# Batch norm factors and bias sums made by GpSimd while the count table is filled, the row factors spread by a matmul in the first pass

## The reference

```python
def _bn(h, gamma, beta, mean, var):
    return (h - mean) * (gamma * jax.lax.rsqrt(var + BN_EPS)) + beta
for i in range(L):                                   # L = 3
    agg = jax.ops.segment_sum(h[src], dst, num_segments=N)
    h = h + agg
    h = jnp.maximum(_bn(h @ W1[i] + b1[i], g[i, 0], be[i, 0], rm[i, 0], rv[i, 0]), 0.0)
    h = h @ W2[i] + b2[i]
    h = jnp.maximum(_bn(h, g[i, 1], be[i, 1], rm[i, 1], rv[i, 1]), 0.0)
```

## Time and profile before

| | us |
|---|---|
| median of 3 runs | 4120.48 (4119.42 to 4122.16) |
| the profiled execution, its own time | 4127.06 |
| its span, first to last instruction | 4125.4 |
| PE busy | 3764.2 (91%) |
| DVE busy | 3059.2 (74%) |
| ACT busy | 2492.8 (60%) |
| POOL busy | 1375.4 (33%) |

### The profile page before, as it was taken

The page is one execution under the profiler, slowest core; times in us unless marked ns, Lnnn a source line. Parts: engine busy times, 40 slices in busy tenths (PEclk is TensorE's granted clock), DMA queues, the critical chain, the costliest instruction groups (busy, mean ns, idle before and its releaser), DMA issues.

```text
span 4125.4 us, 60005 instructions
## 1 busy us (share of the span) xinstructions
PE 3764.2 (91%) x17331; PEld 2941.7 (71%) x17331; DVE 3059.2 (74%) x5526; ACT 2492.8 (60%) x4754; POOL 1375.4 (33%) x2017
## 2 busy tenths in 40 slices
PE   0118889999999999999899999999999999999999
PEld 0116678888888644555688888888888888887887
DVE  9989956576677778877668667766866866786685
ACT  1119956656656787777565655565565565566555
POOL 0011135533545320000361343244244234456624
PEclk9999999999999999999899999999999999999999
DMA  2019964544543322221143344344344334433444
GB/s 63 0 39 365 364 205 124 142 128 125 145 127 105 95 68 77 73 63 54 55 115 108 107 127 120 107 126 123 109 119 124 108 106 128 119 99 105 115 133 135
DMA packets 234210, 489.83 MB, mean 119 GB/s; under 512 B 32579, under 2 KB 100924, under 8 KB 233495
## 3 DMA queue, kind: packets, MB, share of 16 engines
q1 hardware_dynamic: 213084, 432.93, 36.5%
q0 software_dynamic: 7856, 46.93, 3.1%
q10 hardware_dynamic: 12938, 6.05, 0.7%
HBM read 396.99 MB, written 43.87 MB: 107 GB/s over the span
## 4 chain that ended last, share of the span: by engine, by line
PE 50%; issue 0%; POOL 0%; ACT 0%; DVE 0%; ACTq 0%; POOLq 0%
PE ps L2188 40%; PE ps L2306 3%; PE ps L2307 3%; PE ps L2308 1%; PE ps L2309 1%; PE ps L2350 1%; PE ps L2336 0%; PE ps L2292 0%; PE ps L2331 0%; PE ps L2220 0%; PE ps L2226 0%; PE ps L2211 0%; ACT wide L2035 0%; PE ps L2203 0%; POOL inv L2090 0%
## 5 line engine op out<-in xcount | busy, mean ns | idle before, releaser
L2188 PE MATMUL ps<-wide,hi 128*128 128x512 f32 (+2 forms) x5537 | 2138.3, 389 | 26.0 <-issue 11.7
L2188 PE MATMUL ps<-wide,lo 128*128 128x512 f32 (+2 forms) x5537 | 2078.0, 379 | 0.0
L2035 DVE CAST wide<-ring 128x1536 fp32r<-128x1536 uint8 (+2 forms) x1274 | 1310.0, 1028 | 559.7 <-PE ps L2188 555.0
L2188 PEld LDWEIGHTS ps<-wide,hi 128*128 128x128 f32 x5537 | 1042.7, 188 | 230.9 <-issue 33.0
L2188 PEld LDWEIGHTS ps<-wide,lo 128*128 128x128 f32 x5537 | 1044.3, 189 | 186.0
L2035 ACT CAST wide<-ring 128x768 fp32r<-128x768 uint8 (+1 forms) x1274 | 1152.9, 905 | 3.1 <-DMA ring<-count 2.3
L2402 ACT CAST hi<-high 128x128 fp32r<-128x128 f32 x1274 | 381.4, 299 | 993.8 <-PE ps L2188 618.3
L2127 POOL TENSOR_TENSOR lo<-hN,high 128x128 fp32r<-128x128 f32 x686 | 566.2, 829 | 761.1 <-PE ps L2188 468.6
L2127 POOL TENSOR_TENSOR lo<-hB,high 128x128 fp32r<-128x128 f32 x588 | 498.8, 849 | 762.1 <-PE ps L2188 544.8
L2184 PE MATMUL ps<-hN,hB 128*128 128x512 f32 (+1 forms) x1274 | 525.1, 569 | 5.6 <-DVE aggT L2365 4.2
L2395 ACT ACTIVATE hN<-aggT,source_scores 128x512 f32<-128x512 f32 (+1 forms) x637 | 428.7, 695 | 118.0 <-PE ps L2184 86.7
(11 more groups left out here) (248 smaller groups left out, 3499.0 us busy)
## 6 DMA issues: line engine op xcount, KB each, us to landing
ring<-count SPq DMA_DIRECT2D x490, 320.0 KB, 2.9
ring<-count SPq DMA_DIRECT2D x441, 256.0 KB, 2.6
ring<-count SPq DMA_DIRECT2D x490, 224.0 KB, 2.5
wide<-aggT POOLq DMA_DIRECT2D x49, 896.0 KB, 6.5
count<-aggT SPq DMA_DIRECT2D x49, 800.0 KB, 4.2
xN<-in_x ACTq DMA_DIRECT2D x1, 2744.0 KB
out<-xN SPq DMA_DIRECT2D x1, 1064.0 KB
out<-xN SPq DMA_DIRECT2D x1, 896.0 KB
```

What stands on the lines that cost most here:

```text
L2035: return copy(wide[:, g % WIDE_SLOTS, c0:c1].rearrange("p (t u f) -> p t u f", u=2, f=P), rows[:, g % row_slots, c0:c1].rearrange("p (t f ...
L2188: ins = e.matmul(ps[:, c, 0:size], part[:, g % CUT_SLOTS, :], wide[:, g % WIDE_SLOTS, w0:w0 + size], start=k == 0 and part is hi, stop=k = ...
```

## The change

- `norm_rows`, `rows_bn` and its five DMAs are gone, and so are the two Sqrt activations for `roots` on ScalarE. One Sqrt is left, for the first layer norm. ScalarE's wait for the loads of the vectors moves to the end of its stream in the build.
- `factor_work` is gone from VectorE. Its rest runs on GpSimd in the fill, in two parts: `first_factors` (10 instructions) ahead of the DMA of block 6 and `second_factors` (4 instructions) ahead of that of block 14. The inverse root is made with a power and one Newton step in place of Sqrt and reciprocal. After each part GpSimd waits for its last instruction before it issues the next DMA. All but three of the first part's instructions wait for the one before.
- The row factors are made in the first pass. At g = 40 GpSimd writes ones into a free buffer and the identity times factor and times shift into another (a memset, two `tensor_scalar` of 128x128). At g = 42, behind its sums, TensorE multiplies ones by the pair of diagonals (128x256) into PSUM bank 7, which leaves factor and shift along every row. At g = 45 VectorE multiplies the weights with it and copies the shift.
- The first step of the `Leave` layer waits for these results, on TensorE and on VectorE.

```diff
@@ sort_edges @@
-            e.wait_ge(s["rooted"], 3)
+            e.wait_ge(s["rooted"], 1)
             net.rsqrt(ch, inv, mv[:, :, 1], root[:, :], off)
             e.scalar_tensor_tensor(off, mv[:, :, 0], -1.0, inv, ALU.mult, ALU.mult).then_inc(ch.sem, ch.up())
-            factor_work(ch)
...
-            e.wait_ge(s["v"], 16 * (len(vectors) + len(directs)))
-            for out, var in roots:
-                e.activation(out, var, ACT.Sqrt, bias=net.eps[:, 0:1]).then_inc(s["rooted"], 1)
             e.wait_ge(s["dve"], spread_at[0])
             e.activation(root[:, :], mv[:, :, 1], ACT.Sqrt, bias=net.eps[:, 0:1]).then_inc(s["rooted"], 1)
@@ fill_counts, gpsimd @@
+            ch = Count(e, s["pool"])
             for k in range(NB):
+                if k in PREPARE_AT:
+                    prepare[PREPARE_AT.index(k)](ch)
+                    e.wait_ge(ch.sem, ch.n)
                 if k >= EARLY_SLOTS:
                     e.wait_ge(s["summed"], k - EARLY_SLOTS + 1)
                 e.wait_ge(s["out"], groups * k + last_group)
@@ Flow.run, gpsimd, tensor, vector @@
+                    if g == SPREAD_AT and self.spreads:
+                        e.memset(room[1][0][:, 0:P], 1.0).then_inc(s["diagonal"], 1)
+                        for i in (0, 1):
+                            e.tensor_scalar(room[2][0][:, i * P:(i + 1) * P], net.ident[:, :], layers[-2].norm[i], None, ALU.mult)\
+                                .then_inc(s["diagonal"], 1)
...
+                    if g == SPREAD_AT + 2 and self.spreads:
+                        e.wait_ge(s["diagonal"], 3)
+                        e.matmul(ps[:, SOURCE, 0:PAIR], room[1][0][:, 0:P], room[2][0][:, :], start=True, stop=True).then_inc(s["rows_made"], 1)
...
+                    if g == SPREAD_AT + 5 and self.spreads:
+                        w, shift = layers[-2].second
+                        e.wait_ge(s["rows_made"], 1)
+                        e.tensor_tensor(w, ps[:, SOURCE, 0:P], w, ALU.mult).then_inc(s["rows_kept"], 1)
+                        e.tensor_copy(shift, ps[:, SOURCE, P:PAIR]).then_inc(s["rows_kept"], 1)
@@ program @@
+        def pool_inverse_root(ch, y, var, t, m):
+            e, n = ch.engine, var.shape[1]
+            e.tensor_scalar(t, var, LN_EPS, None, ALU.add).then_inc(ch.sem, ch.up()); e.wait_ge(ch.sem, ch.n)
+            e.tensor_tensor(y, t, net.root_power[:, 0:1].to_broadcast([P, n]), ALU.pow).then_inc(ch.sem, ch.up()); e.wait_ge(ch.sem, ch.n)
+            e.tensor_tensor(t, y, y, ALU.mult).then_inc(ch.sem, ch.up())
+            e.tensor_scalar(m, var, LN_EPS, -0.5, ALU.add, ALU.mult).then_inc(ch.sem, ch.up()); e.wait_ge(ch.sem, ch.n)
+            e.tensor_tensor(t, t, m, ALU.mult).then_inc(ch.sem, ch.up()); e.wait_ge(ch.sem, ch.n)
+            e.tensor_scalar(t, t, 1.5, None, ALU.add).then_inc(ch.sem, ch.up()); e.wait_ge(ch.sem, ch.n)
+            e.tensor_tensor(y, y, t, ALU.mult).then_inc(ch.sem, ch.up()); e.wait_ge(ch.sem, ch.n)
+
+        def first_factors(ch):
+            e = ch.engine
+            e.tensor_tensor(b1s[:, :], b1i[:, :], b1h[:, :], ALU.add).then_inc(ch.sem, ch.up())
+            e.tensor_tensor(b2s[:, :], b2i[:, :], b2h[:, :], ALU.add).then_inc(ch.sem, ch.up())
+            e.tensor_copy(att_rep[:, :], w_att[:, 1:2].to_broadcast([P, P])).then_inc(ch.sem, ch.up())
+            pool_inverse_root(ch, bn[:, 1, :], vec[:, 4, :], bn[:, 0, :], bn[:, 2, :])
```

More of the change, by code:

```diff
@@ L211, in sort_edges @@
     inv, off = seen
-    roots, factor_work = factors
     keys_dram = nc.dram_tensor("sorted_keys", [NKEYS], F32, kind="Internal").ap()
@@ L547, in fill_counts @@
     assert len(pieces) == groups == 4
-    names = ["left", "apart", "right", "mm", "out", "spread", "normal", "turned", "state", "high", "hi", "lo", "summed", "whole", "copied",
+    names = ["left", "apart", "right", "mm", "out", "spread", "normal", "turned", "state", "high", "hi", "lo", "summed", "whole", "copied", "pool",
              *[f"loaded{j}" for j in range(EARLY_SLOTS)]]
@@ L924, in _, with build_counts @@
                         e.sem_inc(s["cut"])
-def build_counts(nc, net, src, dst, count, many, loads, factors, stored):
+def build_counts(nc, net, src, dst, count, many, loads, stored, prepare):
     with ExitStack() as ctx:
@@ L936, in build_counts @@
         sort_edges(nc, net, src, dst, many,
-                   (row_of, code_of, sb("order", [P, P], BF16), sb("codes", [P, P], I16), orders_by, marks_by), loads, seen, factors)
-        fill_counts(nc, net, count, (row_of, code_of, orders_by, marks_by), seen, stored)
+                   (row_of, code_of, sb("order", [P, P], BF16), sb("codes", [P, P], I16), orders_by, marks_by), loads, seen)
+        fill_counts(nc, net, count, (row_of, code_of, orders_by, marks_by), seen, stored, prepare)
 class Net:
@@ L1813 @@
 class Leave:
+    norm: tuple
     first: tuple
@@ L1978, in run @@
             "high", "hi", "lo", "wide_act", "wide_dve", "used", "summed", "took_dve", "took_act", "product", "kept",
-            "first", "second", "mid", "gates", "rz", "pre", "new", "next", "dve", "gated", "gate", "weighed", "attended",
+            "first", "second", "mid", "gates", "rz", "pre", "new", "next", "dve", "gated", "gate", "weighed", "diagonal", "rows_made", "rows_kept", "attended",
             "hidden", "relu", "decoded", "biased", "opened", "spread", "pool", "scaled", "biases", "last", "done", "store",
@@ L2236, in _ @@
                             e.wait_ge(s["lv_scored"], scored)
+                        if c.late == 1 and self.spreads:
+                            e.wait_ge(s["rows_kept"], 2)
                         e.matmul(ps[:, 4, 0:c.size], layers[c.layer].first[0], net.aggT[:, c.cols], start=True, stop=True)\
```

42 lines of the change are left out of this document (12 added, 30 removed).

## The result

The changed kernel takes 4144.54 us (4141.11 to 4147.15, 4 runs), the kernel before in the same series 4119.95 (4118.72 to 4122.16). The ratio is 1.006, with an interval of 1.0047 to 1.0072. The forecast was 4119.6, with a range from 4113 to 4124.5. A second series gave 4145.65 against 4120.60, ratio 1.0058 (1.0041 to 1.0075).

A forecast was written before the change was run, and what follows sets the result against it. VectorE was taken to bound build and fill, TensorE the passes. Terms: -6.3 (build) + 4.5 + 0.4 (fill) + 0.5 (pass) = -0.9 us, carried to the median: 4119.6 us, own range 4117 to 4122, with rivals 4113 to 4124.5.

The forecast's parts named there:

- The stalls: Fill: DMAs queued behind GpSimd's small instructions come late; +4.5 us for the first part after VectorE's 1.3 reserve, +0.4 for the second.
- the build: Build: removing VectorE's work between layer norm and keys ends it 6.7 us earlier, less 0.4 for late gathers: -6.3 us.
- The first copy: Build: ScalarE's first key copy ends at 275.27, so VectorE's key group 0 would run from 275.4 to 279.25.
- the wait of group 1: Build: the second key group would wait for ScalarE's second copy until 280.35, where it began at 287.04 before.
- the last one of the sum: Whole kernel: the median lies 6.6 us below the profiled execution, and this difference carries over unchanged, giving 4119.6 us.
- Rival D: Build: gaps between dependent instructions come back in key group 0, gain only 2.9 us; total +2.5, 4123.0 us; chance 0.10.
- the rule: Fill: GpSimd gets in only where a VectorE instruction ends, so the tenth small instruction is done at about 343.0.
- The second part: Fill, ahead of block 14: four chained GpSimd instructions take about 5 us where 4.2 are free; +0.4 us, ends 0 and 1.1.
- C: Fill: GpSimd gets turns only at the ends of lines 584 and 585; stall 14.9 us, total +9.9, 4130.4 us; chance 0.10.
- B: Fill: GpSimd is not shut out by VectorE's 16-bit instructions, stall 0; total -5.8, 4114.7 us; chance 0.27.
- The point from which the change is a loss: Fill: a stall of 5.4 us, with the tenth small instruction done at 343.9, makes the whole change a loss.
- The pass: Passes: one more 128x256 f32 matmul on TensorE costs +0.5 us; GpSimd's three new instructions, 3.7 us together at most, are hidden.

The follow-up runs named there:

- experiment 10: Changed kernel with only row factors by diagonals, column factors and bias sums on VectorE in the build: 4123.22 us against 4127.29; kernel before also rerun unchanged: 4126.43, 4120.64.
- the trace of 4120.15: The kernel before, unchanged, run once more: the one trace of its lower level; that series measured 4120.64 us beside 4119.60.
- experiment 5: Changed kernel with VectorE waiting for its own line 582 ahead of line 583 in blocks 7 and 15 alone: 4127.13 us against 4120.59, ratio 1.0016.
- the version in the sort: Changed kernel with both parts of GpSimd's small instructions moved from the fill into the build's sort: 4120.37 us against 4120.59; second series 4121.21 against 4126.03.

## Why the prediction was wrong

The measured time is 24.9 us above the forecast. The stalls are 19.0 of it (23.9 for 4.5 + 0.4), the build 5.4 (0.9 for 6.3), and the rest is 0.5.

**The build, step by step right, against the wrong base.** The first copy, the wait of group 1, the absence of gaps and the sum of -6.3 (measured -6.18) held against the profiled execution. The step that failed here is the last one of the sum: "The median of the runs lies 6.6 us below the profiled one, and I take the difference over". By experiment 10 most of the difference was the gaps that the prediction itself had marked as unexplained in the earlier trace rows. That the runs of the median had none is inferred from the trace of 4120.15; they left no traces. Against such a run the build wins 290.22 - 289.33 = 0.9 us, not 6.2. A difference of 6.6 us between a profile and a median whose runs spread over 2.7 should have been traced to a row before it was carried over. Rival D was half right: the gaps come back in group 0 when instructions stand ahead of the keys (experiment 10). What makes them in some series and not in others stays open. The changed kernel and all its variants without work on VectorE there showed none, so the change does take the upper level away.

**The stall: the rule was right, its reach wasn't.** This is the step that cost most. "So GpSimd gets in only where a VectorE instruction ends" was drawn from rows in which VectorE had gaps shortly before, as everywhere in the passes. There it holds, and the working from it was close: with the door opened once (experiment 5) the tenth instruction is done 13.0 us after the DMA of block 5 (336.19 - 323.2; forecast 343.0 - 329.4 = 13.6), and the stall is 5.1 us (forecast 4.7). The last agreement is partly luck: the DMA was 342.83 - (343.60 - 6.15) = 5.4 us late for 6.0, and only 0.3 came off for 1.3. In a stream of back-to-back instructions 8.1 us and more behind the last gap it doesn't hold, and 4.7 became 13.41 us. The second part, forecast at 0.4 us, lost 10.51 by the same cause, since it has a first instruction too. The page "SBUF — State Buffer" of the Trainium skill (section "Who interferes with whom") says that the engine that issues first has the shared pair of ports for the whole instruction, and the other is blocked. The addition that 19 finished instructions pass by (18.76 us) is outside this rule. The same section says that a VectorE instruction with two SBUF inputs does not hold up a GpSimd instruction that only writes, and here the trace agrees (memset, 0.22 us beside line 582).

**Two smaller terms of the stall.** Block 6's DMA landed 4.1 us after its issue (346.08 to 350.15) and not 6.5, and TensorE came back slower, at a granted clock of 0.75 from 350.15 to 362, that is with half of the stretch at 1.2 GHz (0.76 us for the form of matmul that takes 0.47 at 343.60). From the landing to VectorE's start it takes 5.1 us. The lateness is 350.15 - (343.60 - 6.18) = 12.7 us, so only 0.7 is added where 1.3 should have come off.

**The rivals.** C was on the right side, with a stall of 14.9 us, but by another mechanism: turns at two of the five ends. Experiment 5 shows turns behind short instructions too. B (no lock-out) is refuted by every trace with reading instructions in the fill. C's sum takes 0.8 us for the second part, which its own working puts at 0.4. The point from which the change is a loss was put at a stall of 5.4 us. Against the runs of the median it is at 0.4.

**The pass was right:** 0.46 us for 0.5. GpSimd's instructions took 2.1 us beside a bound of 3.7.

**What follows for the change:** without the stall it is worth 0.9 - 0.46 = 0.4 us where the kernel before has no gaps, which can't be measured (0.9991 to 1.0010 for the version in the sort), and 3 to 6 us where it has them. No version here beats the kernel before in every series.

## What to carry to other kernels

Don't queue a small GpSimd instruction that reads SBUF ahead of a DMA on which others wait, in a stretch where VectorE runs back to back: its price is not its length, but how long VectorE can run without a gap. Where it must stand there, one wait of VectorE on its own last instruction, 0.04 us of idle time shortly ahead, was enough to let a whole chain in; the chain still took 13 us and stalled VectorE for 5.1. Behind the last DMA or in the sort the same instructions cost nothing that could be measured. And explain the distance between the profiled execution and the median by a row before a sum is carried from one to the other: it may be the very term that the change removes.

## What the runs showed of the hardware

- GpSimd's first reading instruction in a gapless stretch of VectorE, a `tensor_tensor` of 128x3 or 128x6, waited 15.10 to 18.95 us in all ten places where it was tried, past up to 19 ends of VectorE's instructions, until VectorE stopped. After a gap of 0.04 us, requests 2.4 and 3.3 us later were served at the next end; one 8.1 us later was not. A memset took 0.22 us there, beside a `tensor_tensor` of VectorE.
- A chain of dependent VectorE instructions beside the last gathers of the build shows waits of 0.2 to 1.6 us between them in two traces and none in a third, of the same program: the 22 instructions end 5.5 us later in the earlier trace rows (11.5 us for 6.0).
- A power of six columns takes 1.37 us on GpSimd; the estimate was 1.3.
- GpSimd's issue of a gather takes 1.12 to 1.20 us instead of 0.94 beside VectorE's instructions on the int32 keys (275.50, 277.00 and 278.50 in the changed kernel).
